# Attention in a six-stage kernel: the projection of q and k one head earlier on TensorE, its copies one exponential earlier on ScalarE

## The reference

```python
qkv = layernorm(x) @ W_attn + b_attn          # q, k, v: 16 heads of 8 channels
att = einsum('bhtd,bhsd->bhts', q, k) / sqrt(8) + rel_bias
att = softmax(where(causal, att, -inf))
y = einsum('bhts,bhsd->bhtd', att, v)
x = x + y @ W_proj + b_proj
```

## Time and profile before

| | |
|---|---|
| median of three runs | 1420.02 us (1418.97 to 1423.3) |
| span of the profiled execution | 1415.3 us |
| median less span | 4.7 us |
| PE busy in the span | 1301.7 us, 92% |
| attention on PE | about 69 to 385 us of the span |
| TensorE clock granted, mean | 0.964 |

### The profile page before, as it was taken

One profiled execution on the slowest core, in us unless ns is written; L12 is line 12 of the kernel. 1 busy time (PEld: TensorE's weight loads), 2 busy tenths in 40 slices (PEclk: granted clock), 3 DMA queues, 4 the chain that ended last, 5 costly groups with the idle time before them and its releaser, 6 DMA issues. The chain is left out here.

```text
span 1415.3 us, 35725 instructions
## 1 busy us (share of the span) xinstructions
PE 1301.7 (92%) x10556; PEld 1109.4 (78%) x10556; DVE 958.2 (68%) x4074; ACT 783.4 (55%) x1882; POOL 780.1 (55%) x1027
## 2 busy tenths in 40 slices
PE   6789999999786788999978999999999979999998
PEld 5567777777575577888867999999888867888887
DVE  5557676767486774556545787888878858566564
ACT  2257777777625533444424766676667654444443
POOL 2167777777434174555533556566577663344453
PEclk9989999999976999999988999999999999999999
DMA  5199930000033011221112122122122102222221
GB/s 154 41 273 272 271 97 0 0 0 1 6 105 108 12 66 34 29 31 29 29 22 52 50 50 53 45 52 50 48 57 60 42 27 71 51 29 30 30 30 15
DMA packets 102600, 85.67 MB, mean 61 GB/s; under 512 B 10504, under 2 KB 90090, under 8 KB 102203
## 3 DMA queue, kind: packets, MB, share of 16 engines
q1 hardware_dynamic: 83796, 65.90, 16.9%
q0 software_dynamic: 17280, 16.17, 6.5%
q10 hardware_dynamic: 1382, 1.83, 0.5%
HBM read 21.32 MB, written 45.78 MB: 47 GB/s over the span
## 5 line engine op out<-in xcount | busy, mean ns | idle before, releaser
L1909 POOL TENSOR_TENSOR attn_z<-attn_top,attn_z 128x256 f32<-128x256 f32 x256 | 155.9, 618 | 60.1 <-DVE attn_top L1856 60.1
L1856 DVE CUSTOM_DVE_ANT_0 attn_z<-banks,rel_bias 128x128 f32<-128x128 f32 (+1 forms) x512 | 148.5, 353 | 42.1 <-PE banks L2004 40.6
L2386 POOL TENSOR_TENSOR ret_rotated<-ret_twins 128x512 f32<-128x512 f32 x64 | 82.1, 1284 | 134.3 <-DVE ret_twins L2296 134.1
L1942 ACT ACTIVATE attn_prob<-banks 128x384 f32<-128x384 f32 x256 | 119.2, 492 | 7.2 <-PE banks L2014 2.4
L930 DVE SCALAR_TENSOR_TENSOR moe_block_act<-banks,moe_block_weights,moe_block_gated 128x128 f32<-128x128 f32 x276 | 77.7, 344 | 64.2 <-ACT moe_block_gated L985 39.4
L2449 ACT ACTIVATE ret_normed<-banks,ret_head_shift,ret_head_rstd 128x128 f32<-128x128 f32 x256 | 96.5, 459 | 44.0 <-DVE ret_head_shift L2320 43.5
L1475 DVE SCALAR_TENSOR_TENSOR moe_block_act<-banks,moe_block_weights,moe_block_gated 128x128 f32<-128x128 f32 x276 | 77.7, 344 | 62.9 <-ACT moe_block_gated L1569 38.9
L2014 PE MATMUL banks<-ident,attn_z 128*128 128x128 f32 x768 | 109.0, 278 | 0.7 <-ACT attn_prob L1942 0.7
L2014 PEld LDWEIGHTS banks<-ident,attn_z 128*128 128x128 f32 x768 | 84.4, 141 | 14.4 <-issue 14.1
L2481 PE MATMUL banks<-ret_x_hi,ret_hi 128*128 128x256 f32 x256 | 85.1, 332 | 1.9 <-ACT ret_gate L2442 1.0
L1522 POOL DMA_INDIRECT out<-moe_block_y,moe_taken x37 | 58.5, 1581 | 47.8 <-ACT moe_block_y L1579 39.7
(11 more groups left out here) (367 smaller groups left out, 4248.6 us busy)
## 6 DMA issues: line engine op xcount, KB each, us to landing
slots<-moe_pad SPq DMA_DIRECT2D x12, 2560.0 KB, 23.4
ret_twins<-ret_twins SPq DMA_DIRECT2D x256, 64.0 KB, 2.0
moe_stage<-in_moe_w SPq DMA_DIRECT2D x4, 576.0 KB, 5.9
bias_reversed<-scratch SPq DMA_DIRECT2D x1, 2048.0 KB, 9.0
y_rows<-moe_pad SPq DMA_DIRECT2D x1, 2048.0 KB, 8.8
back_of_seq<-y_rows SPq DMA_DIRECT2D x16, 128.0 KB, 2.3
out<-x_res SPq DMA_DIRECT2D x8, 256.0 KB, 2.4
ret_stage<-in_ret_w SPq DMA_DIRECT2D x16, 96.0 KB, 2.1
```

The source lines that it names most:

```text
L1856: last = dve.tensor_tensor_reduce(out=z[:, s, cols], in0=ps_s[:, i, cols], in1=bias, scale=1.0, scalar=-3.0e38, op0=ALU.add, op1=ALU.max, ...
L1909: pool.tensor_tensor(z[:, s, P:WIDTH], top[:, s, 1:2].to_broadcast([P, WIDTH - P]), z[:, s, P:WIDTH], ALU.subtract).then_inc(shifted1, 1)
L1942: act.activation(prob[:, slot(k, i), :], ps_p[:, i % 2, 0:WIDTH], ACT.Exp, scale=-1.0).then_inc(prob_ready, 1)
L2386: pool.tensor_tensor(rotated[:, k % 2], twins[:, k % 2, 0], twins[:, k % 2, 1], ALU.add).then_inc(rotated_ready, 1)
```

## The change

The order of two stages is changed in two lists. Nothing is added or removed: each step issues the same instructions with the same waits.

```diff
@@ ACT queue @@
-                (3, copy_avT), (4, of_head(0, exponent)), (4, of_head(1, exponent)), (6, copy_qk), (4, of_head(2, exponent)),
+                (3, copy_avT), (4, of_head(0, exponent)), (6, copy_qk), (4, of_head(1, exponent)), (4, of_head(2, exponent)),
@@ PE queue @@
-                (5, scores), (3, attend), (4, of_head(0, transpose_z)), (4, of_head(1, transpose_z)), (6, project_qk),
+                (5, scores), (3, attend), (4, of_head(0, transpose_z)), (6, project_qk), (4, of_head(1, transpose_z)),
```

## The result

| | before | after |
|---|---|---|
| median | 1419.49 us (4 runs) | 1454.90 us (4 runs, 1451.07 to 1457.50) |
| span of the profiled execution | 1415.3 us | 1455.4 us |
| 62 steps of the attention | 292.6 us | 330.4 us |
| one step, mean | 4.72 us | 5.33 us |
| PE busy, 200 to 240 us | 39.19 us | 33.78 us |

The kernel became slower: the ratio of the times is 1.0236, with a 95% interval from 1.0194 to 1.0278. The profiled execution of the changed kernel had a device time of 1457.16 us of its own, 1.8 us over its span.

The account below looks back on a forecast made before the run. PE's queue was taken to set the pace (busy 39.19 of 40 us). 62 steps x 0.61 = 37.8 us, less 0.9 hidden, gave 36.9 us on the 1420.0 median: 1456.9 us, range 1445 to 1472.

Parts of the forecast that it names:

- Projection moved up by 0.33, for nothing: On PE, the projection ahead of head 1's transposes ends 0.33 us earlier at no cost, its operands being ready.
- Copies and the exponential behind them: On ACT, copy of k ends 0.33 us earlier; head 1's exponential waits behind the copies and ends at 259.81.
- The wake-up of 0.38 us: From the releasing ACT instruction's end to head 3's first transpose's end: 0.38 us, bounds 0.33 and 0.44.
- The small job of four matmuls: On PE behind transpose_heads: ends 0.13 us apart rather than 0.11, making that step's growth 0.62 us.
- The rule of the Trainium skill: If head 3's weight load were done during the wait, about 3 us less in sum; judged unlikely, 0.38 kept.
- The sum: Whole kernel: 62 steps at 0.61 us give 37.8 us, less 0.9 us hidden, so 36.9 us slower.
- What gives back: In 11 steps the scores' wait for DVE's bias is hidden by the longer step: 0.9 us back.
- Attend and the division: DVE's division behind transpose_heads needs 0.65 us before attend on PE; expected hidden with 0.37 us to spare.
- The clock rival: PE's idle 0.7 us per step drops its clock to 1.2 GHz; 26 us on top, 1483 us; chance 8%.
- The other two rivals: Head 3's transposes find their buffer free, 1404 us, 4%; or new wait about equals old, near 1420, 3%.
- My list of signs: Waits list: L2014's weight loads held by exponential L1942 some 60 times, 0.6 to 0.8 us; none held by L1931.

Follow-up runs that it names:

- the last experiment: Kernel before the change with only DVE's normalise moved ahead of the first head's bias; 1423.22 us, ratio 1.0028.
- the dose experiment: Changed kernel with head 1's exponential placed between the copies of q and k on ACT; 1433.05 us, ratio to before 1.0125.
- PE's half alone: Kernel before with only PE's list changed, projection right behind head 0's transposes, ACT's order as before; 1445.14 us, ratio 1.0152.
- ACT's half alone: Kernel before with only ACT's list changed, copies ahead of head 1's exponential, PE's order as before; 1477.61 us, ratio 1.0385.

## Why the prediction was right

The forecast of 1457 us is 2 us off the measured 1454.9, and its mechanism is what the trace shows. By its steps, each time counted from the scores of the 38th step (255.56 before, 278.17 after):

| | predicted | measured |
|---|---|---|
| head 0's transposes end | 2.21 | 2.20 |
| projection ends | 2.91 | 2.91 |
| copies start | 3.03 | 3.02 |
| head 1's exponential ends | 4.25 | 4.24 |
| head 3's transposes end | 4.85 | 4.91 |
| small job ends | 5.29 | 5.34 |
| next scores | 5.22 | 5.27 |

- *Projection moved up by 0.33, for nothing*: right. None of its own waits appears in the list.
- *Copies and the exponential behind them*: right in order and to 0.01 us in this step. In five steps of eight the copies start 0.08 us earlier than forecast, but they did so before the change too, so the growth of a step is not touched by it.
- *The wake-up of 0.38 us* is the term that was mis-sized. From the exponential's end (282.41) to the first transpose's end (283.08 - 0.22 = 282.86) it is 0.45, just past the upper bound of 0.44 that the tail gave. The weight load starts 0.12 after the release, where the small job's did 0.05 after. So the steady steps with a small job of two matmuls grew by 0.65 to 0.68 us (where no hole was lost), not by 0.60.
- *The small job of four matmuls*: the forecast kept their distance of 0.13. No longer released by a wait of their own, they go at 0.11 (277.79 to 278.24 for all four, one step earlier), which takes back 0.06. These steps grew by 0.60 to 0.63 us, as forecast, because two errors cancel; that is luck.
- *The rule of the Trainium skill* ("TensorE: Matmul & The Clock Gate", Part 3, The mechanism: weight loads are pulled ahead of in-flight matmuls) gives nothing here. The first weight load of head 3 starts at 282.53, after the release, and is not drawn into the wait; the trace and the prediction agree that this load, which has a wait of its own, stays behind it.
- *The sum*: 36.9 us expected, 37.9 measured in the trace of the attention, 35.4 between the medians.
- *What gives back*: right in size, wrong in cause. The five steps with a transpose of x that ended in a hole grew by 0.46 to 0.48 us, the other steady ones of this kind by 0.65 to 0.67, and the hole ahead of the scores is gone; but it was not a wait for DVE, as the last experiment shows.
- *Attend and the division*: hidden, as expected. Attend comes at 284.31, 1.01 us after `transpose_heads` has ended (283.30), where 0.65 was needed.
- *The clock rival* is excluded. PE stood for 0.75 to 0.83 us in each step, and the changed kernel's clock was granted in full:

```profile
200.00:240.00 40.00, 33.78 (x402) 26.23 (x401) 24.91 (x152) 28.39 (x75) 28.67 (x56) 1.00 0.00 0
```

The second failure mode that the same page of the Trainium skill tells of (Part 1, A second HAM failure mode), a clock that swings under many short idle times, is not seen at this size of gap. The other two rivals needed the exponential to end 0.6 to 0.7 us earlier and fell with it; the dose experiment shows what half of that would have been worth.

My list of signs said that the waits of L2014 would be put down to the exponential; most weight loads were put down to POOL. The mechanism was right and the sign was badly chosen: I should have said which time of release to look for, rather than which name.

## What to carry to other kernels

In a queue written by hand, what counts of a stage is how much work of its engine lies between the instruction that feeds another engine and the one that wants the answer back. Moving a stage forward takes its cover away from what it covered: here 0.70 us of projection had hidden two exponentials, and a two-buffer tile turned that into a wait of 1 us in every step, to win 0.36. Before reordering, list for each answer the cover it has and the cover it needs; work that needs nothing of its own step (attend, here) is what to put where cover is short.

## What was unexpected of the hardware

- The delay from one engine to another was not one number. From the projection's last matmul to the copies it was 0.11 to 0.13 us in three consecutive steps of each eight and 0.03 to 0.05 in the other five, at the same places of the loop in each kernel whose copies wait for PE; the steps of the kernel before that have the longer delay take 0.07 to 0.08 us more. What makes it is open. From ACT's end to the first weight load that it released it was 0.05 us for the small job (259.76 to 259.81 before) and 0.12 for the transposes. Ends of matmuls in the profile are modelled, but the start of the dependent copy and the length of the step move with it.
- A hole of 0.19 us ahead of the scores once in eight steps, which the list puts down to DVE, stays when DVE is done 0.5 us earlier. It is there in PE's half alone too (0.20) and with head 3 last (0.15), where the small job ahead of it waits for the copy of k as before. It is gone in the changed kernel, in ACT's half alone and with attend behind the transposes, where the small job doesn't wait. The two go together; which causes which was not tried.
- The two halves of the change together cost less than half of their sum (37.9 against 79.5 us).
